# A fused cross-attention and expert layer: the gates' sum and reciprocal move ahead of two residual subtractions on VectorE

## The reference

```python
x = x + jnp.tanh(g_xattn[0]) * xattn(layernorm(x), ctx_1024, Wq, Wkv, Wfc, fc_b, qn_w, kn_w)
x = x + jnp.tanh(g_ffn[0]) * ffn(layernorm(x), Wr, We)
# xattn: q, k rms-normed per head (4 heads of 64), attn = softmax(q k / 8), attn @ v @ Wfc + fc_b
# ffn: logits = x Wr; the two best of 8 experts; w = softmax(top 2 logits);
#      a token beyond an expert's capacity is dropped; out = sum over the two of w * (x We[e])
```

## Time and profile before

| | |
|---|---|
| time before, median of 3 runs | 1363.23 us (1363.19 to 1363.48) |
| the profiled execution | 1363.08 us |
| its span, first to last instruction | 1361.4 us |
| mean granted TensorE clock | 0.993 |
| PE busy | 1330.9 us (98%) |
| DVE busy | 1004.9 us (74%) |
| ACT busy | 873.7 us (64%) |
| POOL busy | 771.9 us (57%) |

### The profile page before, as it was taken

The page is one execution under the profiler, slowest core; times in us unless marked ns, Lnnn a source line. Parts: engine busy times, 40 slices in busy tenths (PEclk is TensorE's granted clock), DMA queues, the critical chain, the costliest instruction groups (busy, mean ns, idle before and its releaser), DMA issues. The chain is left out here.

```text
span 1361.4 us, 27025 instructions
## 1 busy us (share of the span) xinstructions
PE 1330.9 (98%) x7848; PEld 1123.7 (83%) x7848; DVE 1004.9 (74%) x2959; ACT 873.7 (64%) x2529; POOL 771.9 (57%) x997
## 2 busy tenths in 40 slices
PE   8699999999999999999999999999999999999998
PEld 6678888888888888888888888888888888888876
DVE  6677777777777777777787777787777787777763
ACT  5666676666676666676666676666666666666642
POOL 4445555655555655555655565655565655565644
PEclk9889999999999999999999999999999999999999
DMA  6411112211112211111211112212111211111100
GB/s 199 142 40 57 32 54 62 61 43 58 33 52 62 62 41 58 35 51 61 61 43 59 41 43 62 61 42 61 44 39 61 61 43 59 45 26 47 31 16 24
DMA packets 106835, 73.92 MB, mean 54 GB/s; under 512 B 67776, under 2 KB 85120, under 8 KB 106688
## 3 DMA queue, kind: packets, MB, share of 16 engines
q1 hardware_dynamic: 106688, 72.20, 17.7%
HBM read 40.25 MB, written 31.92 MB: 53 GB/s over the span
## 5 line engine op out<-in xcount | busy, mean ns | idle before, releaser
L382 PE MATMUL bkM<-we,x2T 128*128 128x512 f32 x3072 | 792.4, 401 | 0.9 <-DVE ctx_sb L1264 0.9
L382 PEld LDWEIGHTS bkM<-we,x2T 128*128 128x128 f32 x3072 | 551.8, 188 | 121.0 <-ACT a_out L854 7.5
L854 ACT ACTIVATE a_out<-bkM,gate 128x256 f32<-128x256 f32 x512 | 216.2, 479 | 155.2 <-PE bkM L382 153.9
L1264 DVE SCALAR_TENSOR_TENSOR ctx_sb<-bkM,gate,ctx_sb 128x256 f32<-128x256 f32 x384 | 184.7, 481 | 101.8 <-PE bkM L382 90.2
L632 POOL TENSOR_TENSOR a_sum<-a_sum,a_out 128x256 f32<-128x256 f32 x256 | 188.3, 736 | 119.0 <-ACT a_out L854 87.4
L619 POOL TENSOR_TENSOR probs<-probs,p_inv 128x308 f32<-128x308 f32 x128 | 89.6, 700 | 213.9 <-DVE p_inv L1157 213.9
L573 POOL TENSOR_TENSOR rstd<-ve,minus_half 128x4 f32<-128x4 f32 x64 | 65.1, 1017 | 145.2 <-DVE ve L1048 142.5
L573 POOL TENSOR_TENSOR q_r<-q_ve,minus_half 128x8 f32<-128x8 f32 x64 | 105.3, 1646 | 54.0 <-DVE q_ve L1142 54.0
L731 ACT ACTIVATE xn<-x_sb,shift,rstd 128x256 f32<-128x256 f32 x124 | 64.5, 591 | 77.4 <-DVE shift L1057 77.4
L637 POOL TENSOR_TENSOR ctx_sb<-a_sum,ctx_sb 128x256 f32<-128x256 f32 x128 | 94.8, 740 | 17.0
L815 ACT ACTIVATE probs<-bkA,s_bias,q_r 128x77 f32<-128x77 f32 x128 | 51.4, 412 | 74.0 <-DVE s_bias L1152 74.0
(11 more groups left out here) (202 smaller groups left out, 2583.1 us busy)
## 6 DMA issues: line engine op xcount, KB each, us to landing
x_sb<-in_x SPq DMA_DIRECT2D x32, 512.0 KB, 3.9
out<-ctx_sb SPq DMA_DIRECT2D x64, 256.0 KB, 2.2
v_rows<-v_nat SPq DMA_DIRECT2D x38, 256.0 KB, 2.3
kd<-kT_rows SPq DMA_DIRECT2D x128, 38.5 KB, 2.4
vf<-v_rows SPq DMA_DIRECT2D x128, 38.5 KB
kT_rows<-kT_sb SPq DMA_DIRECT2D x38, 128.0 KB, 2.1
ctx_late<-in_ctx SPq DMA_DIRECT2D x28, 128.0 KB, 3.7
stage<-in_L_ffn_We SPq DMA_DIRECT2D x2, 1024.0 KB, 6.4
```

The lines of the kernel that those rows point to most:

```text
L382: mm = nc.tensor.matmul(out, l, r, start=(i == 0), stop=(i == len(terms) - 1))
L854: ins = nc.scalar.activation(a_out[:, t % 2, (e // 4) * 2 + i], bkM[1][:, i * D:(i + 1) * D], ACT.Copy, scale=gate[:, m.parity, t, e:e + 1])
L1264: nc.vector.scalar_tensor_tensor(out=acc_v[:, t], in0=bkM[0][:, i * D:(i + 1) * D], scalar=gate[:, m.parity, t, e:e + 1], in1=src, op0=ALU ...
```

## The change

The first two instructions of `gates`, with the wait for egap before them, become a function of their own, `gates_sum`. In a step it is called in slot 13, ahead of the low halves of tiles 0 and 1. The rest of `gates` stays in slot 14. In the second round it is called where it was.

```diff
--- before.py
+++ after.py
@@ -1215,6 +1215,12 @@
                     did(nc.vector.tensor_tensor(both[:], mask[:, 0], mask[:, 1], ALU.add))
                 assert steps[0] == (ROUTE_HALF, ROUTE_STEPS)[i]
 
+            def gates_sum(p):
+                dve.wait_ge(egap_done.sem, egap_done.at(p))
+                nc.vector.tensor_scalar(den[:], egap[:], 1.0, None, ALU.add).then_inc(gate_chain.sem, 1)
+                dve.wait_ge(gate_chain.sem, gate_chain.at(p, 1))
+                nc.vector.reciprocal(w_top[:, 0], den[:]).then_inc(gate_chain.sem, 1)
+
             def gates(p):
 
                 def did(ins):
@@ -1223,10 +1229,6 @@
                 def bc(a):
                     return a.unsqueeze(2).to_broadcast([P, T, E])
 
-                dve.wait_ge(egap_done.sem, egap_done.at(p))
-                did(nc.vector.tensor_scalar(den[:], egap[:], 1.0, None, ALU.add))
-                dve.wait_ge(gate_chain.sem, gate_chain.at(p, 1))
-                did(nc.vector.reciprocal(w_top[:, 0], den[:]))
                 dve.wait_ge(gate_chain.sem, gate_chain.at(p, 2))
                 did(nc.vector.tensor_tensor(w_top[:, 1], w_top[:, 0], egap[:], ALU.mult))
                 did(nc.vector.tensor_tensor(g_part[:, 0], mask[:, 0], bc(w_top[:, 0]), ALU.mult))
@@ -1336,9 +1338,12 @@
                     chunk(k, m, p)
                     if f:
                         inverse(f, 3)
-                if k == 13 and f:
-                    pT_part(f, 0)
-                    pT_part(f, 1)
+                if k == 13:
+                    if p:
+                        gates_sum(p)
+                    if f:
+                        pT_part(f, 0)
+                        pT_part(f, 1)
                 if k == 14:
                     if p:
                         gates(p)
```

## The result

| | before | changed |
|---|---|---|
| median of 4 runs each | 1363.21 us (1362.98 to 1363.48) | 1352.56 us (1351.82 to 1353.38) |
| the profiled execution, its span | 1363.08, 1361.4 us | 1352.05, 1350.3 us |

The ratio is 0.9923, with a 95% interval of 0.9911 to 0.9935: faster by 10.6 us. (The 4 runs before are the 3 of the first table and one more.) I had predicted 1355.4 us in a range from 1354.0 to 1360.0. The direction was right, and the gain was larger than the 7.8 us of the sum, outside the range.

A forecast was written before the change was run, and what follows sets the result against it. TensorE, busy 1330.9 us of 1361.4 us, was taken as the bound. Saving 0.26 us in 30 steps gives 7.8 us: 1363.08 - 7.8 = 1355.3, with 0.15 for the runs' median 1355.4 us, range 1354.0 to 1360.0.

The forecast's parts named there:

- the 7.8 us of the sum: At the second `attend` of slot 15: 0.26 us a step saved on TensorE, times 30 steps.
- Which wait, and who ends it: Weight loads for bkC, second `attend` of slot 15: idle 15.2 us in all, ended by VectorE's low half of tile 3.
- The new place is free: Behind inverse(f, 3): `den` (0.16 us) and the reciprocal fit VectorE's idle 0.74 us, with 0.45 us left; no cost.
- the lost race: In the new place, `den` is issued after POOL's normalise and sits it out; harmless if it waits for that alone.
- the 0.31 of the rival: `den` waits for normalise alone: tile 1 0.31 us late, inside 0.45, still 1355.4 us; chance 0.78 together with the forecast.
- The old place, 0.87 us won, the wait inherited by w_top: In the gates chain w_top takes 0.70 instead of 0.62 us; tile 3's low half is out 0.87 us earlier.
- The whole 0.26 us is saved, not more: Six expert matmuls ahead of the second `attend` take 1.39 instead of 1.65 us, in each of 30 steps.
- One such place that comes back in every step: The list of waits shows only one recurring TensorE wait: weight loads for bkC, 30 times, 15.2 us in all.
- Nothing is taken back later: Later slots keep the saving; the rival, half of it lost to VectorE or ScalarE chains, 1359.3 us, had chance 0.09.
- The range: 1354.0 to 1360.0 us; low end from 0.6 us of reading error and as much for small shifts elsewhere.
- The slower rival: `den` sits out normalise and the following POOL addition; first `attend` 0.56 us later, step 0.30 us longer, 1372 us; chance 0.07.
- Its point of decision: The slower rival takes hold once the low half of tile 1 is over 0.45 us late.

The follow-up runs named there:

- late087: The changed kernel with three idle VectorE reductions (256, 256, 128 elements, about 0.87 us) ahead of tile 2's low half in each of the 30 steps; 1362.54 us.
- behind_norm: The changed kernel with one idle VectorE reduction of 160 elements (about 0.24 us) between inverse(f, 3) and `den`; 1353.75 us.
- den_psum: The kernel before, in its old order, with `den` written to unused columns of bkC in PSUM and waiting for the positions; 1355.50 us.
- wtop_early: The changed kernel with the product into w_top also moved up, behind the reciprocal; 1352.32 us.
- late kernels: The changed kernel with idle VectorE reductions of about 0.53, 0.65 or 0.87 us ahead of tile 2's low half; 1353.78, 1355.83 and 1362.54 us.
- behind_add: The changed kernel with three idle VectorE reductions of 256 elements between inverse(f, 3) and `den`; 1364.31 us.
- behind_two: The changed kernel with idle VectorE reductions of 256, 256 and 128 elements (about 0.87 us) between inverse(f, 3) and `den`; 1352.05 us.

## Why the prediction was right, and where it was wrong

- **Which wait, and who ends it:** right. The wait of 15.2 us at bkC was VectorE's lateness with tile 3, though the profile wrote "issue". late087 brought it back by delaying VectorE alone.
- **The new place is free:** right, to 0.01 us. `den` came 0.16 us ahead of normalise and took 0.14 us, and tiles 0 and 1 stayed. behind_norm showed that even the lost race would have been free (tile 1 was 0.15 us late there, not the 0.31 of the rival, since tile 0 does not wait for the reciprocal's end).
- **The old place, 0.87 us won, the wait inherited by w_top:** right (5.37 to 4.50). den_psum and wtop_early showed the inheritance twice more.
- **"The whole 0.26 us is saved, not more":** this is the step that failed. The saving was 0.37 us a step. The mechanism was right; the term of the sum, 0.26 us a step, was too small. 30 times the missing 0.11 is 3.3 us; the runs came out 2.8 us below the forecast. I measured the wait from the six matmuls ahead of it, to the first start of the `attend` behind, and took the rest of the idle 0.51 us for a lead that costs nothing. A first matmul whose load was late is recorded 0.03 us behind the load, one whose load was early 0.23. So 0.20 of the 0.46 us looked free, but the `attend` itself then took 1.49 instead of 1.38 us. The late kernels put the free part at about 0.1 us. The number was in the trace of the kernel before: 1.49 for the twelve matmuls behind the wait, 1.41 for those of `fc`. The first `attend`, with 694.43 - 692.93 = 1.50 us, made 1.49 look usual; it follows transposes, and it too lacks a lead.
- **"One such place that comes back in every step":** a misreading without harm. The list of weight-load waits has four more with 30 to 32 times each, 8.6 us at bkC (`positions`), 7.5 at bkM, 6.6 at bkB and 5.8 at another load for bkC. They are 8.6, 7.6, 6.4 and 5.7 us in the changed kernel. That the clock was low in the last slice can't be read from the earlier trace rows either, where it is a 9; the trace has it low for the last 3 us.
- **Nothing is taken back later:** right; all that lies outside the six and the twelve matmuls changed by 0.01 us a step.
- **The range:** its low end allowed 0.02 us a step for the reading of the wait, 0.6 us in all, and about as much again for the rest. That covers an error of reading within the chosen rows; it leaves no room for rows that were chosen too narrowly.
- **The slower rival:** a mechanism that exists (behind_add), 0.96 us of delay away. Its point of decision was right: tile 1 could be 0.45 us late, was 0.85 late (2.62 against 1.77), and the load for bkF came 0.40 late. Its price was not: a step of 40.78 us where 40.75 + 0.30 = 41.05 was worked out. Tile 1 came 0.16 us earlier than I had it (2.62 against 693.39 - 690.61 = 2.78), since tile 0 starts ahead of the reciprocal's end, and the wait saved at bkC was 0.37 instead of 0.26.

## What to carry to other kernels

Price a wait of TensorE by the whole groups on both sides of it: here the matmuls behind it were slower as well, and the sum was lateness less 0.1 us. Where a small VectorE instruction takes 0.6 us instead of 0.15, set it beside POOL's rows: here such instructions ended with a POOL instruction each time. What follows in line may inherit the wait, so count from the POOL instruction's end, not from the duration saved. Moving it into VectorE's idle time, or sending its result to PSUM, gave the same steady step here.

## What the runs showed of the hardware that was not expected

- A load for bkC 0.11 us late cost 0.02 us a step; beyond that the price rose about one for one (0.25 late, 0.13; 0.44 late, 0.32; 0.46 late, 0.37).
- An addition of constant 1.0 to four numbers took 0.70 us with its result in SBUF and 0.15 us with its result in PSUM, both begun about 0.05 us behind the start of the same POOL instruction.
- `den` began 0.003 us behind a POOL addition by the records, while POOL's normalise was still at work, and took 0.16 us (behind_two). Begun 0.04 us behind normalise and 0.14 us behind the addition it took 0.68 and 0.63 us (behind_norm, behind_add). Which of closeness and the earlier instruction decides is open.
- A product whose one input is a broadcast waited for POOL like any other with two inputs in SBUF (0.72 instead of 0.18 us).
